# Mixer of a four-batch perceiver block: input products from GpSimd to VectorE, half of the state sums to TensorE, and the context's two fp32r words handed on through DRAM

## The reference, cut to what matters

```python
x = x + _L0_xattn_ref(_layernorm(x), ctx_1024, ctx_1024, mask, ...)   # one head of 1024, context 4 x 4096 x 256
x = x + _L0_attn_ref(_layernorm(x), ...)                              # selective scan
x = x + _L0_ffn_ref(...)                                              # soft mixture of experts
x = x + _L1_xattn_ref(_layernorm(x), ctx_1024, ctx_1024, ...)         # 16 heads; K, V from the same context
x = x + _L1_attn_ref(...)
x = x + _L1_ffn_ref(...)

# inside _L0_attn_ref, 512 channels d, 16 states n:
dA = exp(einsum('bld,dn->lbdn', delta, A))
dBu = einsum('bld,bln,bdl->lbdn', delta, B, u)
carry = a * carry + bu
y = einsum('bdn,bn->bd', carry, c)
```

## Time and profile before

| | |
|---|---|
| median of 3 runs | 2279.72 us (2273.21 to 2279.77) |
| the profiled execution | 2274.87 us, of which its span is 2273.4 us |
| busy share of the span | TensorE 83%, VectorE 75%, ScalarE 52%, GpSimd 29% |
| mean granted TensorE clock | 0.908 of full speed |
| wide cross attention | 0 to 315 us |
| mixer, to its first scan | 315 to 430 us |
| mixer, unit loop | 430 to 901 us |
| mixer, out-projection | 901 to 920 us |
| the rest | 920 to 2273 us, untouched by the change |

### The profile page before, as it was taken

The page is one execution under the profiler, slowest core; times in us unless marked ns, Lnnn a source line. Parts: engine busy times, 40 slices in busy tenths (PEclk is TensorE's granted clock), DMA queues, the critical chain, the costliest instruction groups (busy, mean ns, idle before and its releaser), DMA issues. The chain is left out here.

```text
span 2273.4 us, 33815 instructions
## 1 busy us (share of the span) xinstructions
PE 1897.6 (83%) x13021; PEld 1293.5 (57%) x13021; DVE 1714.7 (75%) x1890; ACT 1190.8 (52%) x2053; POOL 663.0 (29%) x477
## 2 busy tenths in 40 slices
PE   7999979666676766499999689999999999998554
PEld 5787755444454543378787545555555555555324
DVE  6767535799999999455664389888888988845685
ACT  1333325843455332343442058888888888883271
POOL 3422111566665753122221001111010111106322
PEclk8999989977789777799999879999999999998776
DMA  8466334454444443311210332423333333301000
GB/s 280 148 223 216 118 89 124 156 173 153 152 154 158 146 156 116 100 42 57 79 61 3 101 94 85 118 81 116 95 102 95 102 104 92 89 11 51 14 1 18
DMA packets 139117, 242.89 MB, mean 107 GB/s; under 512 B 9408, under 2 KB 83648, under 8 KB 131536
## 3 DMA queue, kind: packets, MB, share of 16 engines
q1 hardware_dynamic: 137232, 240.26, 33.5%
q10 hardware_dynamic: 1728, 0.49, 0.1%
HBM read 169.41 MB, written 71.30 MB: 106 GB/s over the span
## 5 line engine op out<-in xcount | busy, mean ns | idle before, releaser
L1976 DVE TENSOR_REDUCE xn_peaks<-psum 128x2 f32<-128x1024 f32 x512 | 622.2, 1225 | 98.7 <-PE psum L1824 94.6
L1941 ACT ACTIVATE xn_weights<-psum 128x512 f32<-128x512 f32 x1024 | 552.7, 597 | 61.2 <-PE psum L1829 17.6
L1824 PE MATMUL psum<-xn_k_words,xn_q_words 50*128 50x512 f32 x1024 | 376.7, 460 | 8.5 <-DVE xn_peaks L1976 7.3
L1829 PE MATMUL psum<-xn_q_words,xn_k_words 50*128 50x256 f32 x2048 | 377.0, 307 | 3.5 <-ACT xn_weights L1941 2.5
L1829 PEld LDWEIGHTS psum<-xn_q_words,xn_k_words 50*128 50x128 f32 x2048 | 249.7, 186 | 195.2 <-ACT xn_weights L1941 163.0
L1860 PE MATMUL psum<-xn_weights,xn_v 128*32 128x256 f32 x4096 | 327.9, 392 | 1.7 <-issue 0.3
L1109 DVE TENSOR_TENSOR_SCAN mx_state<-mx_decay,mx_state 128x1024 f32<-128x1024 f32 x64 | 213.8, 3341 | 0.0
L1824 PEld LDWEIGHTS psum<-xn_k_words,xn_q_words 50*128 50x128 f32 x1024 | 186.9, 188 | 18.8 <-DVE xn_peaks L1976 16.5
L870 POOL TENSOR_TENSOR mx_state<-mx_du,mx_b_all_channels 128x1024 f32<-128x1024 f32 x64 | 177.5, 2774 | 0.7
L1038 ACT ACTIVATE mx_decay<-mx_delta,mx_a 128x512 f32<-128x512 f32 x128 | 85.3, 715 | 169.4 <-DVE mx_state L1109 169.4
L695 PE MATMUL psum<-ctx_k_words,ctx_minus_identity 128*128 128x512 f32 x64 | 41.3, 645 | 120.5 <-ACT ctx_k_words L738 120.5
(11 more groups left out here) (332 smaller groups left out, 3321.8 us busy)
## 6 DMA issues: line engine op xcount, KB each, us to landing
xn_k_words<-k_words SPq DMA_DIRECT2D x128, 400.0 KB
k_words<-ctx_k_words SPq DMA_DIRECT2D x192, 256.0 KB
v_all<-ctx_v SPq DMA_DIRECT2D x32, 544.0 KB, 3.5
xn_v<-v_all SPq DMA_DIRECT2D x32, 544.0 KB, 4.2
xw_mask<-in_mask_BxSxS_ik SPq DMA_DIRECT2D x8, 2048.0 KB, 8.5
xw_ctx_natural<-in_ctx SPq DMA_DIRECT2D x32, 512.0 KB, 5.9
ctx_chunk<-in_ctxT SPq DMA_DIRECT2D x32, 512.0 KB, 4.0
moe_w<-in_L_ffn_w SPq DMA_DIRECT2D x16, 1024.0 KB, 5.4
```

The costliest lines, as they stand in the source:

```text
L1824: return pe.matmul(PS[:, 2 * (x % 2) + a, :], t["Q"][narrow_rows(a), m % XN_QSLOTS, q * P:(q + 1) * P], K[narrow_rows(a), m % XN_KSLOTS, c ...
L1829: return pe.matmul(PS[:, narrow_bank("exp", n, step, a), half * S:(half + 1) * S], K[narrow_rows(a), n % XN_KSLOTS, kt * P:(kt + 1) * P], ...
L1941: act.activation(t["weights"][:, step % 4, a, :, :], bank.rearrange("p (t s) -> p t s", t=2), ACT.Exp, scale=XN_SCALE).then_inc(s.taken, 1)
L1976: dve.tensor_reduce(t["peaks"][:, m % 2, q, :, c], PS[:, 2 * (x % 2):2 * (x % 2) + 2, :], AX.X, ALU.max).then_inc(s.top_read, 1)
```

## The change

- GpSimd no longer makes the unit's product du x B; VectorE does (`inputs`), one unit ahead, between the scan and the product with C.
- Only every second unit's two halves are added by VectorE (`mx_added`, in `added`, after the next unit's scan). For the others TensorE adds both halves with two products.
- The wide stage stores both words of every context chunk to a DRAM tensor `ctx_words` as soon as they are split (`store_words`), and VectorE waits for all stores of a batch before it overwrites `ctxT`. The context projection loads the two words (2 x 512 KB a chunk) in place of the raw context; ScalarE's high and GpSimd's low word there are gone.
- The copies of values out of PSUM move from VectorE to ScalarE.
- The 15 early context steps all lie in the delta phase (`mx_early`: 4, 8, 12, 15), none between the in-projections; there the logarithm of a tile follows the next tile's exponential.

```diff
+    def store_words(b, c):
+        sp.wait_ge(s.ctx_hi, CH * b + c + 1)
+        sp.wait_ge(s.ctx_lo, CH * b + c + 1)
+        for a in range(2):
+            sp.dma_start(k.ctx_words[b, a].rearrange("(k p) s -> p k s", p=P)[:, :, c * BANK:(c + 1) * BANK],
+                         t["ctxT"][:, c, a, :, :].bitcast(F32)).then_inc(s.stored, 16)
...
     for c in range(CH):
-        sp.wait_ge(s.ctx_hi, c + 1)
-        sp.wait_ge(s.ctx_lo, c + 1)
+        store_words(0, c)
         load_rows(0, c)
...
-            if j % QT == 0 and b + 1 < B and c + XW_RAW < CH:
-                sp.wait_ge(s.ctx_hi, CH * (b + 1) + c + 1)
-                sp.wait_ge(s.ctx_lo, CH * (b + 1) + c + 1)
-                load_words(b + 1, c + XW_RAW)
+            if j % QT == 0 and b + 1 < B:
+                store_words(b + 1, c)
+                if c + XW_RAW < CH:
+                    load_words(b + 1, c + XW_RAW)
+    sp.wait_ge(s.stored, 32 * CH * B)
...
         if b:
             dve.wait_ge(s.scores, CH * (QT * b - 1) + c + 1)
+            dve.wait_ge(s.stored, 32 * CH * b)
...
     def fetch(i):
-        sp.dma_start(t["chunk"][:], d["ctxT"][i // CH].rearrange("(k p) s -> p k s", p=P)[
-            :, :, i % CH * BANK:(i % CH + 1) * BANK]).then_inc(s.chunk, 16)
+        for a in range(2):
+            sp.dma_start(t["loaded"][:, i % 2, a, :, :], k.ctx_words[i // CH, a].rearrange("(k p) s -> p k s", p=P)[
+                :, :, i % CH * BANK:(i % CH + 1) * BANK]).then_inc((s.in0, s.in1)[i % 2], 16)
...
-        if sub == 0 and i + 2 < CTX_CHUNKS:
-            sp.wait_ge(s.hi, i + 2)
-            sp.wait_ge(s.lo, i + 2)
-            fetch(i + 2)
+        if sub == 0 and 0 < i < CTX_CHUNKS - 1:
+            sp.wait_ge(s.vp, 2 * i)
+            fetch(i + 1)
...
+    def values(i, pair):
+        act.wait_ge(s.vp, 2 * i + pair + 1)
+        if i:
+            act.wait_ge(s.vs, 16 * i)
+        else:
+            act.wait_ge(s.v_ones, 1)
+        for j in range(2):
+            last = act.copy(t["V"][:, :, 2 * pair + j, :, 0:XN_DH],
+                            k.PS[:, banks[2 + pair], j * D:(j + 1) * D].rearrange("p (r a n) -> p r a n", a=2, n=XN_DH))
+        last.then_inc(s.vc, 1)
...
+        parts = 1 if mx_added(i) else MX_NQ
+        for j in range(parts):
+            last = pe.matmul(PS[:, 4 + group % 2, :], k.ident[:], t["state"][:, i % MX_STATES, j, :],
+                             start=(q + j == 0), stop=(q == MX_NU - 1 and j == parts - 1))
+        last.then_inc(s.sum, 1)
...
+    for m in range(DT):
+        sizes(m)
+        if m:
+            logarithm(m - 1)
+        ctx.upto(mx_early(m))
+    logarithm(DT - 1)
...
+    def inputs(i):
+        half, m, q = mx_unit(i)
+        dve.wait_ge(s.du, i // MX_NU + 1)
+        dve.wait_ge(s.spread, 2 * MX_NQ * (half * MX_NU + q + 1))
+        if i >= MX_STATES:
+            dve.wait_ge(s.sum, i - MX_STATES + 1)
+        dve.tensor_tensor(t["state"][:, i % MX_STATES, :, :],
+                          t["du"][:, m % 2, None, :].to_broadcast([P, MX_NQ, MX_HALF]),
+                          t["Bb"][:, q * MX_NQ:(q + 1) * MX_NQ, :], ALU.mult).then_inc(s.bin, 1)
...
+        if i and mx_added(i - 1):
+            added(i - 1)
+        if i + 1 < MX_UNITS:
+            inputs(i + 1)
         dve.wait_ge(s.scan, i + 1)
-        dve.wait_ge(s.spread, 2 * MX_NQ * (half * MX_NU + q + 1))
         dve.tensor_tensor(h, h, t["Cb"][:, q * MX_NQ:(q + 1) * MX_NQ, :], ALU.mult).then_inc(s.cmul, 1)
```

More of the change, by code:

```diff
@@ L196, in wide_sems @@
                      "small ctx_hi ctx_lo scores filled kept peak neg exp total rinv turned et_act et_dve z_pe z "
-                     "zt_pe zt o_pe x m_pe m row_pe row plus", clear)
+                     "zt_pe zt o_pe x m_pe m row_pe row plus stored", clear)
     return s, k.sem_row("xw_ctxT", CH, clear), k.sem_row("xw_ctxN", CH, clear)
@@ L751, in step @@
             rounded(i, 1, 1)
-    return Steps(step)
-def context_dve(k, t, sems, banks):
-    s, dve = sems[0], k.dve
-    def step(n):
-        i, pair = n // 4, n % 4 - 2
-        if pair < 0:
-            return
-        dve.wait_ge(s.vp, 2 * i + pair + 1)
-        if i:
-            dve.wait_ge(s.vs, 16 * i)
-        else:
-            dve.wait_ge(s.v_ones, 1)
-        for j in range(2):
-            last = dve.tensor_copy(t["V"][:, :, 2 * pair + j, :, 0:XN_DH],
-                                   k.PS[:, banks[2 + pair], j * D:(j + 1) * D].rearrange("p (r a n) -> p r a n", a=2,
-                                                                                         n=XN_DH))
-        last.then_inc(s.vc, 1)
+            values(i, 0)
+        else:
+            values(i, 1)
     return Steps(step)
@@ L795, in mx_bank, with mx_early, mx_added @@
     return (1, 4, 5, 0)[n % 4]
+def mx_early(m):
+    return min(4 * (m + 1), MX_EARLY)
+def mx_added(i):
+    return i % 2 == 1
 def mx_context(point):
@@ L865, in prepare @@
         pool.memset(starts, 0.0).then_inc(s.start, 1)
-        pool.wait_ge(s.du, i // MX_NU + 1)
-        pool.wait_ge(s.spread, 2 * MX_NQ * (half * MX_NU + q + 1))
-        if i >= MX_STATES:
-            pool.wait_ge(s.sum, i - MX_STATES + 1)
-        pool.tensor_tensor(t["state"][:, i % MX_STATES, :, :],
-                           t["du"][:, m % 2, None, :].to_broadcast([P, MX_NQ, MX_HALF]),
-                           t["Bb"][:, q * MX_NQ:(q + 1) * MX_NQ, :], ALU.mult).then_inc(s.bin, 1)
-    for new in range(MX_UNITS):
-        ctx.upto(mx_context(2 * new + 1))
-        prepare(new)
-        if new >= MX_AHEAD:
-            ctx.upto(mx_context(2 * new + 2))
-    ctx.upto(CTX_STEPS)
+    for i in range(MX_UNITS):
+        prepare(i)
 def mixer_pe(k, t, s, ct, cs):
@@ L1006, in mixer_act, with sizes @@
     act.activation(t["A"][:], t["A"][:], ACT.Exp).then_inc(s.aexp, 1)
-    for m in range(DT):
+    def sizes(m):
         lo = 4 * (m % 2)
         e, w, lw = t["elw"](m)
-        ctx.upto(2 * DT - 1 + 2 * m + 1)
         act.wait_ge(s.delta_pe, m + 1)
@@ L1126, in gated @@
         dve.tensor_tensor(t["U"][:, m, tokens], t["U"][:, m, tokens], t["gate"][m][:, tokens], ALU.mult).then_inc(s.g, 1)
-    for i in range(-MX_AHEAD, MX_UNITS + MX_BEHIND):
-        new = i + MX_AHEAD
-        ctx.upto(mx_context(2 * new + 1))
-        if 0 <= i < MX_UNITS:
+    inputs(0)
+    for i in range(MX_UNITS + MX_BEHIND):
+        if i < MX_UNITS:
             recur(i)
-            ctx.upto(mx_context(2 * new + 2))
+        elif i == MX_UNITS and mx_added(i - 1):
+            added(i - 1)
         if i >= MX_BEHIND and (i - MX_BEHIND) % MX_NU == MX_NU - 1:
```

64 lines of the change are left out of this document (21 added, 43 removed).

## The result

The changed kernel takes 2193.0 us (median of 4 runs, 2190.75 to 2194.79); the kernel before took 2278.2 us beside it on the same chip (4 runs). The ratio is 0.9629, 95% interval 0.961 to 0.9648: 85 us faster, 20 us under the forecast of 2213 us and inside its range. The profiled execution took 2194.79 us, its span is 2193.5 us, 80 us under that of the kernel before.

A forecast was written before the change was run, and what follows sets the result against it. VectorE was taken to bound the unit loop, TensorE the wide stage. 2274.87 + 26 (wide stage) + 4 (stretch ahead of the loop) - 92 (loop) = 2213 us, range 2168 to 2260.

The forecast's parts named there:

- the floor of 349 us: Unit loop: VectorE's own work, 64 units of 5.15 us plus gating and du products, 122 us less than 470.6.
- spread units: Unit loop: in sixteen units with spread copies ScalarE needs 6.25 us against VectorE's 5.32, adding 15 us.
- lockstep: Unit loop: the TensorE chain, barely hidden behind VectorE, adds 0.2 us to each of the 48 other units, +10 us.
- new waits: Unit loop: VectorE's input products and gating wait for sums of earlier units, 5 us in all (0 to 15).
- The rival with a new ScalarE-TensorE chain: Unit loop: that chain is the new bound at 6.6 us per unit, loop 422 us, kernel 2257 us; chance 0.20.
- the loop's -92: Unit loop: 349 + 15 + 10 + 5 = 379 us against 470.6; ends -122 and -45.
- The stretch ahead of the loop: Mixer before the first scan: in-projections -8.5, delta phase +17 and +6, first scan -10.7; sum +4 us (-10 to +18).
- The wide stage: Wide cross attention: loads wait behind new stores, 8 us at three batch changes, plus 2 for a mask; +26 us (0 to 60).
- The stores hide: Whole kernel: VectorE's floor is reached and the wide stage's stores cost nearly nothing, 2162 us; chance 0.15.
- slower by the stores: Wide stage: a stored byte costs the DMA engines twice a loaded one, kernel 2294 us; chance 0.06.
- VectorE isn't freed: Unit loop: VectorE's long durations belong to its instructions themselves, loop 520 us, kernel 2355 us; chance 0.04.
- the prediction's other estimate: Unit loop: each of eight GpSimd du products costs VectorE its whole 2 us, 16 instead of 8, sum 2221 us.

The follow-up runs named there:

- the pair of useless instructions: Changed kernel plus, in each unit, a GpSimd instruction nobody waits for: a subtraction that reads SBUF, 2260.0 us, or a memset that only writes, 2193.9 us.
- without context steps: Changed kernel with the 113 context steps of the scan loop moved behind it: 2499.1 us (one run), first to last scan 316.1 us.
- late gating: Changed kernel with VectorE's gating of each group of states four units behind the scan instead of two: 2192.5 us.
- all additions: Changed kernel with VectorE adding the two halves of every unit's product, not of every second unit: 2192.0 us.
- the stores alone: Kernel before with only the wide stage's stores of context words and the waits for them added, nobody reading the words: 2293.1 us.

## Why the prediction was right, and where it wasn't

*What bounded the loop before, and the removal.* Right, and shown by the pair of useless instructions: VectorE's long durations were the price of GpSimd's reading. My 150 us lost to 280 us of GpSimd work are 0.54 us per us, where the experiments gave 0.57 and 0.70. VectorE is busy 145 us less in the loop. By the groups of the earlier trace rows and those after, the scans give 67 us, the product with C 48, the additions (fewer and shorter) 56 and the copies of values 40, and the new product takes 77; the rest is gating and closer starts. The copies' 40 us are read from the earlier trace rows; no run puts them back alone. My unit of 5.15 us was 0.4 us too dear, 25 us over the loop: I took 1.26 us for the product and 2.32 for the scan from a stream in which each waited for its neighbour; interleaved they take 1.13 and 2.20. That is the mis-sized term behind the floor of 349 us, which measured about 320.

*What is added to the floor.* Here the step failed, though the size nearly fits. I had VectorE as the bound with 30 us on top (spread units 15, lockstep 10, new waits 5). There are 40 us on top, half of them in the 16 units with spread copies (11 in units 0 to 7, 9 in units 32 to 39), not most; 26 of the 40 lie ahead of the seven gatings. Even those in the spread units are not of ScalarE's copies alone, for without context steps VectorE doesn't wait there either. The 40 us belong to the context steps: VectorE's waits can be moved (late gating), traded for work (all additions), and only go when the steps go. The rival with a new ScalarE-TensorE chain, to which I gave 0.20, had the right place; its 6.6 us a unit were 5.7. I had costed TensorE's part at 11.2 us a chunk and the transfers at 9.5, "hidden", each by itself; the chain in which a rounding waits for a store takes 12.2 with nothing else running. The two errors have opposite signs: the floor was 29 us too high, and what lies above it 10 us too low. That the loop's -92 came as near to -110 as it did is in part luck.

*The stretch ahead of the loop.* +11 instead of +4. The in-projections gave 6.7 us for my 8.5, and the first scan follows its decays as forecast, at 1.6 us:

```profile
455.05 1.22 DVE L1102 TENSOR_TENSOR mx_state<-mx_du,mx_b_all_channels 128x1024 f32<-128x1024 f32 x1
457.07 2.29 DVE L1112 TENSOR_TENSOR_SCAN mx_state<-mx_decay,mx_state 128x1024 f32<-128x1024 f32 x1 [0.81 <-POOL mx_decay L854]
```

The eight steps more in the delta phase cost 28 us (17.7 + the 10.6 of the scan's wait) for my 23.

*The wide stage.* The mechanism was right and its size too large: +16 for +26. The queue moved 379 GB/s in the full window, not the 340 that I had scaled from a share of 0.80, and the casts behind a pair of stores and a load came 3.85 us apart for my 4.65 (379 GB/s alone would make it 4.15); and the first copy was 6.4 us late for my 8.

*The other rivals.* "The stores hide" is refuted by the stores alone; "slower by the stores" needed a wide term over 88 us and got 16; "VectorE isn't freed" is refuted by the mean of the scan. Gating and du together took 320.6 - 64 x 4.75 = 17 us for my 11 + 8; the gating's own rows are 11 us, so that the eight products for du cost about 6, not 8, and not the 16 of the prediction's other estimate.

## What to carry to other kernels

Work that a second engine does "for free" in SBUF has to be priced by what it does to the others: the useless instruction test, one that reads and one that only writes, gives that price in two runs. When a bound engine is freed, add up each remaining chain in its own order, with its stores and their landing, not engine by engine; run the suspected chain with everything else out of its way, and its own pace shows. And behind a change that adds stores, look first at what stands behind them in the queue: the order was worth at least 13 us of this stage.

## What the runs showed of the hardware that I had not expected

A GpSimd subtraction of 2.33 us took 1.63 us from VectorE; a memset of 0.95 us took nothing. Independent neighbours on VectorE start 0.12 to 0.13 us closer than dependent ones: 1.13 for 1.26 us on a 128x1024 product. The changed kernel has both: ahead of its loop three dependent operations on 128x1024 values start at 451.38, 452.64 and 453.90 us, 1.26 us apart, and the independent product behind them at 455.05 us, 1.15 us later.

TensorE's clock: in the loop without context steps (its grouped instructions, 430 to 790 us, have the line below), where TensorE was busy 184 of 316 us and waited 124 us for VectorE between sums, the granted clock was 0.68 of full speed, a mixture of the 1.2 and 2.4 GHz levels, and the same sum's matmul had a mean of 980 ns; in the changed kernel's loop, busy 296 of 361 us, it was 0.96 and the mean 618 ns. The kernel before had 0.81.

```profile
L929 PE MATMUL psum<-mx_state,identity 128*128 128x512 f32 x192 | 163.0, 980 | 123.9 <-DVE mx_state L1125 116.6 <-DVE mx_state L1120 7.3
```
